# A decoder block on one core: where the scan input is multiplied and where the state sum is added up, in the first block only

## The reference

```
dA  = exp(dt_t * A)                  # (batch, 1024 channels, 16 states)
dBx = dt_t * B_t * x_t
h   = dA * h + dBx                   # one step for each of 64 tokens
y_t = sum over the 16 states of h * C_t
y   = (ys + D_param * xc) * silu(z)
out = y @ out_proj_w.T
```

## Time and profile before

| | |
|---|---|
| median of three runs | 2511.42 us |
| the profiled execution | 2514.9 us, its span 2512.9 us |
| TensorE busy | 2072.8 us, 82% |
| VectorE busy | 1796.9 us, 72% |
| ScalarE busy | 1134.6 us, 45% |
| GpSimd busy | 613.1 us, 24% |
| DMA traffic | 310.95 MB, of it 136.33 MB by GpSimd's queue |

### The profile page before, as it was taken

The page is one execution under the profiler, slowest core; times in us unless marked ns, Lnnn a source line. Parts: engine busy times, 40 slices in busy tenths (PEclk is TensorE's granted clock), DMA queues, the critical chain, the costliest instruction groups (busy, mean ns, idle before and its releaser), DMA issues.

```text
span 2512.9 us, 26202 instructions
## 1 busy us (share of the span) xinstructions
PE 2072.8 (82%) x7700; PEld 1220.0 (49%) x7704; DVE 1796.9 (72%) x1800; ACT 1134.6 (45%) x2716; POOL 613.1 (24%) x438
## 2 busy tenths in 40 slices
PE   6700028999999889999999979999999968799997
PEld 2200004456556534445555534445655634688873
DVE  3599964399999964299999965289999964445443
ACT  2644412565656512556556513466655522344430
POOL 0099950001111110001111110001111111565630
PEclk9755559899999999899999989899999989899998
DMA  1289971247777741257776751247777662212110
GB/s 59 85 170 187 192 181 51 79 124 166 160 164 173 149 127 50 84 140 165 164 169 152 162 150 50 68 121 165 169 173 159 152 152 85 72 63 83 63 55 17
DMA packets 98750, 310.95 MB, mean 124 GB/s; under 512 B 11232, under 2 KB 11360, under 8 KB 96640
## 3 DMA queue, kind: packets, MB, share of 16 engines
q0 software_dynamic: 37632, 136.33, 29.0%
q1 hardware_dynamic: 61056, 173.85, 21.6%
HBM read 167.27 MB, written 4.46 MB: 68 GB/s over the span
## 4 chain that ended last, share of the span: by engine, by line
PE 65%; DVE 18%; issue 8%; ACT 4%; DMA 3%; POOL 0%; DVEq 0%; SPq 0%; POOLq 0%; ACTq 0%
PE pq L1375 12%; PE acc L1465 8%; DVE hs L1187 5%; PE pq L1420 5%; PE acc L1322 5%; PE pk L1404 4%; PE pk L1396 3%; PE pk L1441 3%; PE pq L1422 3%; PE acc L1454 3%; DMA xc<-hs 3%; PE pq L1586 3%; PE pq L1367 2%; DVE hs L1015 2%; PE pk L1586 2%
## 5 line engine op out<-in xcount | busy, mean ns | idle before, releaser
L611 POOL DMA_DIRECT2D xc<-hs x192 | 167.0, 919 | 1380.2 <-DVE hs L1022 1007.5
L1015 DVE TENSOR_TENSOR_SCAN hs<-dA,hs 128x1024 f32<-128x1024 f32 x192 | 428.9, 2276 | 0.0
L1465 PE MATMUL acc<-wb,oT 128*128 128x512 f32 x768 | 358.8, 612 | 3.5 <-ACT oT L784 3.5
L796 ACT ACTIVATE dA<-dt,aneg 128x504 f32<-128x504 f32 x384 | 253.5, 709 | 229.2 <-DVE hs L1015 229.0
L1375 PE MATMUL pq<-qT,wa 128*128 128x512 f32 x768 | 347.4, 606 | 2.9 <-DVE sc L1076 2.9
L1022 DVE TENSOR_TENSOR hs<-hs,bc 128x1024 f32<-128x1024 f32 x256 | 308.0, 1205 | 2.2
L1586 PE MATMUL pq<-wb,xc 128*128 128x512 f32 x128 | 68.7, 663 | 278.0 <-DVE xc L1208 274.5
L758 ACT ACTIVATE pr<-sc,mx 128x64 f32<-128x64 f32 x512 | 170.8, 335 | 215.9 <-DVE mx L1082 215.9
L1322 PE MATMUL acc<-xnT,wa 128*128 128x512 f32 x512 | 229.2, 601 | 10.2 <-PE acc L1322 4.8
L1375 PEld LDWEIGHTS pq<-qT,wa 128*128 128x128 f32 x768 | 149.2, 195 | 173.0 <-issue 167.4
L1006 DVE TENSOR_TENSOR hs<-u,bc 128x1024 f32<-128x1024 f32 x192 | 226.1, 1219 | 7.4 <-ACT xc L891 5.9
(11 more groups left out here) (192 smaller groups left out, 3372.3 us busy)
## 6 DMA issues: line engine op xcount, KB each, us to landing
xc<-hs POOLq DMA_DIRECT2D x256, 512.0 KB, 7.0
bc<-bc_rows SPq DMA_DIRECT2D x64, 512.0 KB, 6.8
wa<-in_wq SPq DMA_DIRECT2D x64, 512.0 KB, 7.5
wb<-in_wo SPq DMA_DIRECT2D x64, 512.0 KB, 5.0
wa<-in_wx SPq DMA_DIRECT2D x16, 512.0 KB, 4.7
wa<-in_wz SPq DMA_DIRECT2D x16, 512.0 KB, 3.6
wb<-in_ow SPq DMA_DIRECT2D x16, 512.0 KB, 5.3
wk<-in_wk SPq DMA_DIRECT2D x32, 256.0 KB, 9.6
```

Of the source, the lines that this page charges most:

```text
L796: ins = S.activation(to[:, :, 1:SEQ], dt[:, s, :].rearrange("p (b t) -> p b t", t=SEQ)[:, :, 1:SEQ], ACT.Exp, scale=aneg[:, s, bass.ds(jj ...
L1015: V.tensor_tensor_scan(out=hs[:, c, :], data0=dA[:, c % 2, :], data1=hs[:, c, :], initial=0.0, op0=ALU.mult, op1=ALU.add).then_inc(scd.sem, 1)
L1465: ins = M.matmul(acc[:, t, :], oT[:, h, t * P:(t + 1) * P], wb2(o % 2)[:, h, :], start=False, stop=(stop and h == 1))
```

## The change

Block 0 now takes the path of the other blocks on VectorE and ScalarE: scan input, scan and product with C all on VectorE in `hs`, and the decays in `dA`. GpSimd's part of block 0 is gone, with its 64 products and 64 adding DMAs. The sum over the states is made by TensorE: it clears all eight PSUM banks with a product of zeros, and then adds, for each state and chunk, two products of the identity matrix with a half of the chunk, one for each channel tile. Each such pair increments `y_added`, for which `scan_input` waits before it overwrites the chunk. At the end VectorE adds the eight banks to `xc`, and then multiplies by silu(z) as before. The waits on `s_y` of the later blocks count from 0 instead of from one block's worth.

```
-        def decays(c):
-
-            return (pq if c % 2 == 0 else pk)[:, :, :].rearrange("p d t -> p (d t)")
-
-        inputs = [x[:, :, :].rearrange("p a t -> p (a t)") for x in (qp, qr)]
+        def y_bank(s):
+
+            return acc[:, s, :] if s < TT else bank(s - TT)
...
-                                eng.wait_ge(s_y[d], i * (16 * NS) + jj * 32 + (16 * p + 16))
+                                eng.wait_ge(s_y[d], (i - 1) * (16 * NS) + jj * 32 + (16 * p + 16))
...
-                def feed(jj, p, c, first):
...
-                    G.tensor_tensor(
-                        inputs[c % 2].rearrange("p (d t) -> p d t", t=T), u[:, 2 * c:2 * c + 2, :],
-                        bc[:, p, 0:1, :].to_broadcast([P, 2, T]), ALU.mult).then_inc(inr.sem, 1)
...
-                        to = (dA[:, c % 2, :] if attn else decays(c))[:, d * T:(d + 1) * T].rearrange(
-                            "p (b t) -> p b t", t=SEQ)
+                        to = dA[:, c % 2, d * T:(d + 1) * T].rearrange("p (b t) -> p b t", t=SEQ)
...
-                    V.tensor_tensor_scan(out=hs[:, c, :], data0=decays(c), data1=inputs[c % 2], initial=0.0,
-                                         op0=ALU.mult, op1=ALU.add).then_inc(scd.sem, 1)
...
+                steps(eng, step)
                 if mamba:
                     eng.wait_ge(yad.sem, yad.upto(i, NS * NCH - 1))
                     eng.wait_ge(szr.sem, szr.upto(i, DT_TILES - 1))
+                    if not attn:
+
+                        for s in range(DT_TILES):
+                            V.tensor_tensor(xc[:, s, :], xc[:, s, :], y_bank(s), ALU.add).then_inc(s_ysum, 1)
                     for s in range(DT_TILES):
+                        if not attn:
+                            eng.wait_ge(s_ysum, s + 1)
                         V.tensor_tensor(xc[:, s, :], xc[:, s, :], silu_z(s), ALU.mult).then_inc(yr.sem, 1)
...
+                    eng.wait_ge(szr.sem, szr.upto(i, DT_TILES - 1))
+                    for s in range(DT_TILES):
+                        M.matmul(y_bank(s), zeros[:, 0:P], zeros[:, :], start=True, stop=False)
+
+                    def sum_y(jj, p, tail):
+                        for c in range(NCH):
+                            eng.wait_ge(hcd.sem, hcd.upto(i, NCH * p + c) + jj * (2 * NCH))
+                            for d in range(2):
+                                ins = M.matmul(y_bank(2 * c + d), ident[:, :], hs[:, c, d * T:(d + 1) * T],
+                                               start=False, stop=(tail and p == 1))
+                            ins.then_inc(yad.sem, 1)
+
+                    steps(eng, sum_y)
```

More of the change, by code:

```diff
@@ L229, in build @@
         s_aneg = sem("decay_rates_made")
-        s_gap = sem("first_decays_cleared")
+        s_ysum = sem("first_y_summed")
         ln1 = stage("ln1_variance", 1)
@@ L885, in one @@
                         eng.wait_ge(ur.sem, ur.upto(i, c))
-                        if not attn and c == 0:
-                            eng.wait_ge(s_gap, 2)
                         if c < 2:
@@ L1107, in one @@
                                         ALU.subtract).then_inc(s_actl, 1)
[L1108 to L1113, removed]
                 if mamba:
```

## The result

The changed kernel takes 2572.86 us (median of 4 runs, 2564.22 to 2581.41), against 2513.16 us (2506.32 to 2519.74) for the kernel before on the same chips: 1.0232 times as long, 95% interval 1.0211 to 1.0253. Its profiled execution has a span of 2572.9 us against 2512.9, 60.0 us more. Predicted were 2570 us, 58.6 more than before. GpSimd's busy time over the execution fell by 222.6 us, from 613.1 to 390.5; some 240 were foreseen.

What follows compares the result with a forecast made beforehand. Block 0's scan was taken as paced by VectorE and wholly on the path. Start +0.4, loop +55.9, tail -2.6 and additions +4.95 gave +58.6 us, so 2570 us; range 2559 to 2583.

Steps and rivals of the forecast that it cites:

- What bounds the stage: Block 0's scan: paced by VectorE, GpSimd level with it, wholly on the path; VectorE's gains or losses count one for one.
- Start: Block 0's first scan input on VectorE starts at 122.63, 0.68 us behind ScalarE's D products; +0.4 us.
- Loop: VectorE's 32 pairs of chunks in block 0, 8.90 us each as in block 1: 284.9 us, +55.9 with its fill.
- the old cycle plus one product: VectorE's loop without overlap: 9.36 us a pair, 14.7 us more, about 2585; chance 0.06 together with TensorE pacing the loop.
- Tail: TensorE's last sum behind VectorE's last product: 5.0 us, within 2.7 to 6.1, against 7.62 by DMA; -2.6 us.
- Additions: VectorE's eight additions of the PSUM banks behind the sum, all on the path: +4.95 us.
- Output projection: Block 0's projection on TensorE starts at 422.4 instead of 363.8, +58.6 us, at half clock; all behind it the same.
- TensorE as the pace: Block 0's loop: TensorE takes 4.88 us a chunk against VectorE's 4.45; +27.5 us, about 2597; chance 0.06, shared with unoverlapped cycle.
- The clock that stays up: TensorE keeps full clock through block 0's scan and into the projection: -5.3 us, 2565; chance 0.10.
- Cheap products without GpSimd: VectorE's 128 products in block 0 each save 0.53 us once GpSimd is silent: 2502, 9 us faster; chance 0.01.
- the old cycle of 3.46 us: Block 0 before: one chunk's product with C and scan fill VectorE without a gap, GpSimd's product ending just in time.

## Why the prediction was right

- **What bounds the stage.** That it is wholly on the path and paced by VectorE held: the projection moved by 57.35 us of the 60.0, and doubling TensorE's work changed nothing in the loop.
- **Start.** Predicted 122.63, measured 122.05; ScalarE's release was 0.4 us earlier in this execution (121.56), and VectorE followed it 0.5 us later instead of 0.7.
- **Loop.** Predicted 8.90 a pair and 284.9 in all; measured 8.91, and 407.11 - 122.05 = 285.1. Reading the price from block 1's rows, and not from the old cycle plus one product, was worth 14.7 us.
- **Tail.** Predicted 5.0 within 2.7 to 6.1, measured 4.33. The last burst began at the slow rate at 406.04 and was at the fast one from 409.52, after 3.5 us, where the prediction took 4 to 5.9; TensorE worked until 411.4.
- **Additions.** Predicted 4.95, measured 4.79; the experiment without them moved the projection by 4.4 us.
- **Output projection.** Predicted at 422.4, measured 421.18. The rest behind it was taken as unchanged and was 2.6 us longer, with a lower granted clock in the last block, not by the change's own instructions.
- **What was luck.** The stage came out 1.2 us under its forecast and the rest 2.6 over, so two misses partly cancel. And that the rest came so near to "unchanged" can't be counted as foreseen: the same code took 2132.1 us in the profiled execution without the additions, at a granted clock of 0.95 to 0.97 from 450 to 2480 us against 0.94 to 0.96 in the changed kernel's. The prediction had no term for that. What holds it up is the stage, 57.35 us against 58.6, and the median over several runs.
- **The rivals.** TensorE as the pace fell with the doubled work. The clock that stays up fell too: 0.77 in the loop, 0.54 at the projection's start; its price was 2.6 us for the projection. Cheap products without GpSimd fell: 1229 ns against 1226.
- **What the prediction didn't see.** It said that VectorE had little to gain by GpSimd's silence, and was right; but it took the old cycle of 3.46 us for VectorE's alone, with GpSimd "level with it". The experiments show that this cycle held only because the scan read its decay from PSUM and VectorE's product with C came first. The whole sum on TensorE takes that PSUM away, so the scan input had to leave GpSimd with it: with the input left there the kernel is at 2639, not at 2510. Not tried was the changed kernel's VectorE path with the decays in PSUM, so the decays' place is not priced on its own there.

## What to carry to other kernels

When work is moved onto the engine that paces a stage, take its price from a stretch of the same trace where that engine already does just this sequence; here that was right to 0.2 us in 285. Before a buffer moves from PSUM to SBUF, look for GpSimd operations that read SBUF beside the VectorE operation that uses it, and at which of the two comes first and what is queued behind it. An idle engine helps even by half: TensorE's sum of two chunks in the free banks took away the DMA tail, started the projection 11.4 us earlier, and gave the fastest kernel here (0.993 times before). Compare the stage and not only the whole: the code behind it, unchanged, varied by up to 20 us from one profiled execution to the next.

## What the runs showed of the hardware

A scan of 128x1024 with both inputs in SBUF took 4.43 us beside a GpSimd product and 2.28 without; with one input in PSUM it took 2.28 beside it. A VectorE product of 1.2 us took 4.36 us when one GpSimd product was under way and a second was issued 0.28 us behind it: it waited through both. TensorE did twice the matmuls in 1.29 times the busy time (225.9 against 175.2 us), at a mean granted clock of 0.98 instead of 0.77 and 0.45 us a record instead of 0.68. Behind the same idle gap of 3.18 us, the same 16 records took 3.68 us in one execution, with 0.55 granted, and 1.97 in another, with 1.00.
